# Expert jobs of a four-layer transformer kernel: the first matrices and the biases stand in SBUF, and ScalarE copies a job's matrix by a register

## The reference, cut to what matters

```python
def _L3_ffn_ref(x, Wg, bg, W1, b1, W2, b2):
    x_flat = x.reshape(N * T, d)                      # 2048 x 256, after a layer norm
    probs = jax.nn.softmax(x_flat @ Wg + bg, axis=-1)
    assignments = jnp.argmax(probs, axis=-1)
    h = jnp.einsum('nd,edh->neh', x_flat, W1) + b1[None]
    h = jax.nn.gelu(h, approximate=False)
    eo = jnp.einsum('neh,ehd->ned', h, W2) + b2[None]
    selected = jnp.take_along_axis(eo, assignments[:, None, None], axis=1)[:, 0, :]
    w = jnp.take_along_axis(probs, assignments[:, None], axis=1)
    return (w * selected).reshape(N, T, d)
x = x + _L3_ffn_ref(_layernorm(x, axis=-1), ...)
```

## Time and profile before

| | us |
|---|---|
| median of 3 runs | 1631.82 |
| lowest, highest | 1628.55, 1633.62 |
| the profiled execution | 1627.8 |
| its span in the trace | 1626.1 |

### The profile page before, as it was taken

One profiled execution on the slowest core, in us unless ns is written; L12 is line 12 of the kernel. 1 busy time (PEld: TensorE's weight loads), 2 busy tenths in 40 slices (PEclk: granted clock), 3 DMA queues, 4 the chain that ended last, 5 costly groups with the idle time before them and its releaser, 6 DMA issues.

```text
span 1626.1 us, 26351 instructions
## 1 busy us (share of the span) xinstructions
PE 1441.3 (89%) x9849; PEld 1075.0 (66%) x9849; DVE 1075.7 (66%) x2362; ACT 750.3 (46%) x1256; POOL 116.0 (7%) x168
## 2 busy tenths in 40 slices
PE   7999999878897996798889999999988899899557
PEld 5666666557783443477786878787864677788546
DVE  4456575778877775787766465555458988886344
ACT  2211212257773665476672222222224877788323
POOL 1000000000000000111000000000010001001323
PEclk9999999989998997999999999999998999999779
DMA  9462202320000000000008910000100000000155
GB/s 320 172 207 78 78 1 78 116 97 14 14 3 1 1 1 1 25 14 1 14 2 271 301 41 1 0 1 0 33 7 7 2 7 2 7 29 26 41 182 185
DMA packets 60286, 96.62 MB, mean 59 GB/s; under 512 B 11092, under 2 KB 48973, under 8 KB 59983
## 3 DMA queue, kind: packets, MB, share of 16 engines
q1 hardware_dynamic: 57742, 78.50, 15.0%
q10 hardware_dynamic: 544, 12.16, 2.2%
q0 software_dynamic: 1872, 4.27, 0.7%
HBM read 73.21 MB, written 37.30 MB: 68 GB/s over the span
## 4 chain that ended last, share of the span: by engine, by line
PE 55%; DVE 17%; issue 11%; ACT 6%; DVEq 5%; DMA 2%; SPq 2%; ACTq 1%; POOL 1%; POOLq 1%
PE bank L2013 8%; PE bank L2014 8%; PE bank L1703 7%; PE bank L1681 7%; DVE MB L928 3%; PE bank L1808 3%; DVE plo L946 3%; PE bank L1859 2%; PE bank L1779 2%; PE bank L1741 2%; PE bank L1781 2%; PE bank L1609 2%; PE bank L1812 2%; PE bank L1813 2%; DVE raw L1223 1%
## 5 line engine op out<-in xcount | busy, mean ns | idle before, releaser
L946 DVE TENSOR_TENSOR plo<-e,phi 120x512 f16<-120x512 f32 x256 | 180.0, 709 | 51.0 <-ACT phi L1431 46.9
L1425 ACT ACTIVATE e<-bank 120x512 f32<-120x512 f32 x256 | 150.5, 588 | 45.5 <-PE bank L1813 36.1
L928 DVE TENSOR_REDUCE MB<-bank 128x4 bf16<-128x480 f32 x256 | 156.2, 648 | 13.7 <-PE bank L1781 9.7
L1431 ACT ACTIVATE phi<-e 120x512 f16<-120x512 f32 x256 | 161.3, 630 | 8.6
L1356 ACT ACTIVATE act<-bank,bin 127x512 f32<-127x512 f32 x64 | 43.1, 686 | 167.3 <-DVE dec L758 163.2
L1681 PE MATMUL bank<-xT,winT 128*127 128x512 f32 (+1 forms) x256 | 114.6, 593 | 1.3 <-ACTq L1327 1.3
L1703 PE MATMUL bank<-woutT,msk 128*128 128x256 f32 (+1 forms) x512 | 115.2, 379 | 0.0
L677 DVE TENSOR_SCALAR high<-raw 128x512 int32<-128x512 int32 x96 | 41.0, 427 | 107.9 <-ACT raw L1562 60.8
L1703 PEld LDWEIGHTS bank<-woutT,msk 128*128 128x128 f32 (+1 forms) x512 | 96.9, 190 | 15.4
L2013 PE MATMUL bank<-hah,h1w 128*128 128x512 f32 x256 | 101.3, 396 | 3.3 <-DVE hal L680 3.3
L557 POOL TENSOR_TENSOR veps<-mv,ceps 128x4 f32<-128x4 f32 x32 | 8.8, 276 | 1335.4 <-DVEq L648 1203.0
(11 more groups left out here) (309 smaller groups left out, 3519.3 us busy)
## 6 DMA issues: line engine op xcount, KB each, us to landing
copy_routed<-zeros SPq DMA_DIRECT2D x1, 17028.0 KB
jw<-copy_experts SPq DMA_DIRECT2D x23, 385.0 KB, 3.3
seen<-in_h1T SPq DMA_DIRECT2D x8, 512.0 KB, 7.2
seen<-in_h2T SPq DMA_DIRECT2D x8, 512.0 KB, 4.8
h1w<-copy_h1T SPq DMA_DIRECT2D x1, 4096.0 KB, 16.6
h2w<-copy_h2T SPq DMA_DIRECT2D x1, 4096.0 KB, 15.1
ctxp<-in_ctxT SPq DMA_DIRECT2D x13, 240.0 KB, 2.9
jx<-copy_routed SPq DMA_DIRECT2D x23, 132.0 KB, 3.2
```

Source lines behind the costliest of these rows:

```text
L928: dve.tensor_reduce(MB[:, t, h0 // 8, SK + h0 % 8:SK + h0 % 8 + 4], b[:, 0:4 * SK].rearrange("p (h k) -> p h k", h=4), AX.X, ALU.max).then ...
L946: dve.tensor_tensor(plo[:, g % 3, :], e32[:, g % 3, :], phi[:, g % 3, :], ALU.subtract).then_inc(s.lo, 1)
L1425: act.activation(e32[:, g % 3, :], bank[2 + g % 3][0:SK, :], ACT.Exp).then_inc(s.exp, 1)
L1431: act.activation(phi[:, g % 3, :], e32[:, g % 3, :], ACT.Copy).then_inc(s.phi, 1)
```

## The change

The expert kits in DRAM are gone, and with them `job_weights`. Instead all first matrices, first biases and second biases are loaded to SBUF next to the second matrices, in the same place of SP's list, by four more DMAs (two of 1 MB for the two halves of the first matrices, one of 8 KB in pieces of 8 bytes, one of 1 MB that repeats the second biases over the partitions). They use SBUF whose tenants are done by then.

Per job only the rows are transferred. The second bias is read in place: VectorE reads the expert's number from `jtab` into a register between `jxln` and `jres`, and `jres` reads `second_bias` by it. The first matrix (and first bias) is copied by ScalarE, SBUF to SBUF, to one of three fixed buffers `jw`: `job_first(j+1)` stands behind the gelu of job j-1, reads the expert's number to a register, and issues two copies of 128 x 258 and 128 x 256. TensorE's list in the loop is what it was, with the new names.

```diff
-            for k in range(K2):
-                sp.dma_start(kits[:, :, W1 + k * D:W1 + (k + 1) * D], a["w1e"][:, k * 128:(k + 1) * 128, :]).then_inc(Hf.zeroed, 16)
-            sp.dma_start(kits[:, :, B1:B1 + K2], a["b1e"].rearrange("p (e k) -> e p k", e=NE)).then_inc(Hf.zeroed, 16)
-            sp.dma_start(kits[:, :, B2:B2 + D], a["b2e"].unsqueeze(1).broadcast_to([NE, 128, D])).then_inc(Hf.zeroed, 16)
         for k in range(K2):
             sp.dma_start(experts[:, :, k, :], a["w2e"][...]).then_inc(ld_experts, 16)
+            sp.dma_start(firsts[k][:, :, 0:D], a["w1e"][:, k * 128:(k + 1) * 128, :].rearrange("e p n -> p e n")).then_inc(ld_experts, 16)
+        sp.dma_start(firsts[0][:, :, D:D + K2], a["b1e"].rearrange("p (e k) -> p e k", e=NE)).then_inc(ld_experts, 16)
+        sp.dma_start(second_bias[:], a["b2e"].unsqueeze(0).broadcast_to([128, NE, D])).then_inc(ld_experts, 16)
-        def job_weights(j, e):
-            sp.dma_start(jw[:, j % NB, :], kits[ds(e, 1), :, :].rearrange("e p n -> (e p) n")).then_inc(ld_job[j % NB], 16)
-            job_weights(j, sp.value_load(jtab[0:1, 1, j:j + 1], min_val=0, max_val=NE - 1))
...
             dve.tensor_scalar(jxln[:, b, :], jx[:, b, 0:D], ...)
-            dve.scalar_tensor_tensor(out=jres[:, b, :], in0=jw[:, b, B2:B2 + D], scalar=jx[:, b, D:D + 1],
+            e = dve.value_load(jtab[0:1, 1, j:j + 1], min_val=0, max_val=NE - 1)
+            dve.scalar_tensor_tensor(out=jres[:, b, :], in0=second_bias[:, ds(e, 1), :].rearrange("p o n -> p (o n)"),
...
+        def job_first(j):
+            if j >= NW:
+                act.wait_ge(Hf.act, j - NW + 1)
+            e = act.value_load(jtab[0:1, 1, j:j + 1], min_val=0, max_val=NE - 1)
+            for k in range(K2):
+                act.activation(jw[k][:, j % NW, :], firsts[k][:, ds(e, 1), :].rearrange("p o n -> p (o n)"), ACT.Copy)
...
+            job_first(0)
             for j in range(JOBS + 1):
                 if j < JOBS:
                     job_columns(j)
                 if j >= 1:
                     job_gelu(j - 1)
+                if j + 1 < JOBS:
+                    job_first(j + 1)
```

More of the change, by code:

```diff
@@ L40 @@
 OH = (NT - TT - 1, 2 * (NT - TT) - 1 + TT - 1)
-W1, B1, B2, KIT = 0, K2 * D, K2 * D + K2, K2 * D + K2 + D
+NW = 3
+W1ROW = (D + K2, D)
 class Layer:
@@ L176, in build @@
     jtab = put("jtab", [1, 2, JOBS], I32, at)
+    free_at = at[0]
     r2 = max(end1, at[0], r1 + 44192)
@@ L311, in build @@
     at = [r4]
+    second_bias = put("second_bias", [128, NE, D], F32, at)
     jx = put("jx", [128, NB, CELL], F32, at)
-    jw = put("jw", [128, NB, KIT], F32, at)
+    jw = [put(f"jw{k}", [128, NW, W1ROW[k]], F32, at) for k in range(K2)]
     jxln = put("jxln", [128, NB, D], F32, at)
@@ L323, in build @@
     experts = put("experts", [128, NE, K2, D], F32, at)
+    at = [r1]
+    firsts1 = put("firsts1", [128, NE, W1ROW[1]], F32, at)
+    at = [free_at]
+    firsts = [put("firsts0", [128, NE, W1ROW[0]], F32, at), firsts1]
+    assert at[0] <= r2 + 1024
     bank = [es.enter_context(nc.psum_tensor(f"bank{b}", [128, 512], F32)) for b in range(8)]
@@ L365, in build @@
     st_job = [sem(f"st_job{b}") for b in range(NO)]
-    LD_JOB = 2 * 16
+    LD_JOB = 16
+    LD_EXPERTS = (2 * K2 + 2) * 16
     TILES3 = PAIRS * HT
@@ L397, in build @@
     W_COPIED = 5 * 16
-    ZEROED = (1 + K2 + 2) * 16
+    ZEROED = 16
     LD_L2, LD_L3X, LD_L3 = (4 + 3 + 2 * 2 + 2) * 16, 4 * 16, 2 * 16
@@ L403, in build @@
     w_in["f3T"] = nc.dram_tensor("copy_f3T", [HID, D], F32, kind="Internal").ap()
-    kits = nc.dram_tensor("copy_experts", [NE, 128, KIT], F32, kind="Internal").ap()
     xbuf = nc.dram_tensor("copy_routed", [SLOTS, CELL], F32, kind="Internal").ap()
@@ L530, in _ @@
                             (ld_l1, LD_L1), (ld_l2, LD_L2), (mask_ready, (0, 16 * 5, 16 * 9)[sum(phases > q for q in (2, 4))]),
-                            (w_copied, W_COPIED), (ld_h1, PAIRS * LD_SEEN + 64), (ld_h2, 16 if phases > 5 else 0), (ld_experts, K2 * 16),
+                            (w_copied, W_COPIED), (ld_h1, PAIRS * LD_SEEN + 64), (ld_h2, 16 if phases > 5 else 0), (ld_experts, LD_EXPERTS),
                             (ld_l3x, LD_L3X if phases > 6 else 0), (ld_l3, LD_L3 if phases > 6 else 0),
@@ L1285, in job_input @@
                               ALU.mult).then_inc(Hf.norm, 1)
-            dve.scalar_tensor_tensor(out=jres[:, b, :], in0=jw[:, b, B2:B2 + D], scalar=jx[:, b, D:D + 1],
+            e = dve.value_load(jtab[0:1, 1, j:j + 1], min_val=0, max_val=NE - 1)
+            dve.scalar_tensor_tensor(out=jres[:, b, :], in0=second_bias[:, ds(e, 1), :].rearrange("p o n -> p (o n)"),
+                                     scalar=jx[:, b, D:D + 1],
                                      in1=jx[:, b, 0:D], op0=ALU.mult, op1=ALU.add)
@@ L1306, in _ @@
             job_table()
+            dve.wait_ge(Hf.tab, 1)
+            dve.wait_ge(ld_experts, LD_EXPERTS)
             for j in range(JOBS + 3):
@@ L1584, in job_gelu @@
                 last = act.activation(jh[:, j % 3, f, :], bank[j % 2][:, f * 128:f * 128 + 128], ACT.Gelu,
-                                      bias=jw[:, j % NB, B1 + f:B1 + f + 1])
+                                      bias=jw[0][:, j % NW, D + f:D + f + 1])
             last.then_inc(Hf.act, 1)
@@ L1592, in _ @@
             exponentials(1)
+            act.wait_ge(ld_experts, LD_EXPERTS)
+            act.wait_ge(Hf.tab, 1)
+            job_first(0)
             for j in range(JOBS + 1):
@@ L2112, in job_up @@
                 for k in range(K2):
-                    last = pe.matmul(bank[j % 2][:, tok(f)], jw[:, j % NB, W1 + k * D + f * 128:W1 + k * D + f * 128 + 128], jxT[:, j % 3, k, :],
+                    last = pe.matmul(bank[j % 2][:, tok(f)], jw[k][:, j % NW, f * 128:f * 128 + 128], jxT[:, j % 3, k, :],
                                      start=(k == 0), stop=(k == K2 - 1))
@@ L2132, in _ @@
             pe.matmul(bank[0][0:1, 0:NE], onesb[:, 0:1], acc[:, len(ROUTES), :], start=True, stop=True).then_inc(Hf.cnt, 1)
-            pe.wait_ge(ld_experts, K2 * 16)
+            pe.wait_ge(ld_experts, LD_EXPERTS)
             pe.wait_ge(Hf.tab, 1)
```

## The result

| | before | after |
|---|---|---|
| median, us | 1630.57 (6 runs, 1626.87 to 1633.62) | 1616.59 (6 runs, 1614.55 to 1618.8) |
| the profiled execution, us | 1627.8 | 1615.67 |
| its span, us | 1626.1 | 1613.9 |

The ratio after to before is 0.9908, with a 95% interval of 0.9892 to 0.9924. The change makes the kernel faster by 0.8 to 1.1%, some 14 us.

What follows compares the result with a forecast made beforehand. SP's two issues per job were taken to bound the job loop (2.453 us a job). Loop 8.0, start 0.8 and end 0.6 sum to 9.4 us, from 1631.8 to 1622.4 us; range 1618.0 to 1628.0.

Steps and rivals of the forecast that it cites:

- the term for the start: Loop start: second job's rows issued one SP slot (1.1 us) earlier, partly lost to TensorE's low clock; 0.8 us gained.
- the allowance of 0.06 us a job for a tie of VectorE and TensorE: Job loop: both engines at 1.97 us wait for each other and lose at irregularities, so 2.03 us a job.
- the step from the profiled execution to the median: Whole time: median of runs shown lies 4.0 us above the profiled execution, so 9.4 is taken from 1631.8.
- What bounds the kernel before: Job loop: SP's two issues per job set a 2.21 us floor; late landings and buffer waits add 0.24.
- The removed DRAM kits (0): Second layer's feed-forward, first pair: the kits' four copies ran beside busy TensorE; removal gives 0 us, at most 0.1.
- the early loads (0): Last attention: four added DMAs take some 12 to 20 us more, nobody waits; 0 us, bounded by 1.
- VectorE, L = 0.84 and a round of 1.97: VectorE in the loop: the register read makes L, from `jxln` to `jres`, 0.84 us and its iteration 1.97.
- TensorE, 1.97: TensorE in the loop: its list is unchanged, with a floor of 1.97 us a job.
- ScalarE's 1.8: ScalarE in the loop: register read and two copies make its round 1.8 us, at worst 2.1; hidden under 1.97.
- Rows land in 2.5: Row loads in the loop: without kits rows land in 2.5 us, the round may be 1.65; not a bound.
- The end, 0.6: After the loop: a 0.6 gap before U(21) goes, then GpSimd's last stores set the end; 0.6 us gained.
- The rivals: VectorE's read dearer, 1626.9 (0.17); rows late, 1629.4 (0.09); ScalarE bound, 1625.6 (0.08); read waits for empty engine, 1636.2 (0.04).

Runs made afterwards that it cites:

- a_down_half: Kernel after, with TensorE's second matmul of each job doing only the first of its two halves of hidden values (output differs); 1615.01 us, one execution.
- b_kit0_late: Kernel before, with job 0's kit issued after SP's wait for the scatters instead of ahead of it; 1630.9 us, one execution.
- a_extra_kit: Kernel after, plus a second register read and a second, kit-sized DMA (385 KB) per job on SP; 1630.55 us, ratio to before 1.0002.
- b_again2: Kernel before, unchanged, profiled a third time; 1630.42 us.
- b_again3: Kernel before, unchanged, profiled a fourth time; 1629.5 us.
- b_again: Kernel before, unchanged, profiled once more (its second profile); 1628.09 us.
- a_extra_small: Kernel after, plus a second register read and a second DMA of 1 KB per job on SP; 1624.5 us, ratio to before 0.9967.
- a_act_copy2: Kernel after, with ScalarE making each matrix copy twice, the first to buffers nobody reads; 1617.37 us, one execution.

## Why the prediction was right and where it was wrong

The mechanism was right: SP's two issues and the kits' bytes held the loop, and without them TensorE's own list sets the round. Of the 5.8 us between 1622.4 and 1616.59, three things are the main part: the term for the start (0.8, where the profiled executions have 2.4: 1.6), the allowance of 0.06 us a job for a tie of VectorE and TensorE that doesn't exist (1.0), and the step from the profiled execution to the median (3.1).

**What bounds the kernel before: right.** Late rows starved the loop, SP's two slots were its floor. The runs put numbers on both: 2.252 us a job with two slots and hardly any bytes, where the prediction had 2.21 plus 0.24 for everything else.

**The removed DRAM kits (0) and the early loads (0): no cost is shown.** The loads of the first matrices and first biases land 8.7 to 10.2 us after their issue, and that of the second biases, issued at 1468.73, 8.3 after it. So all are there about 18 us after the first issue at 1459.24, some 10 us later than the two alone; the estimate was 12 to 20. SP is done with the issues at 1471.5 instead of 1459.8 and still has some 81 us until the job table, where the earlier trace rows have 92.4. The gate step started 0.5 us later than in the profile of before, but so did the first of these issues, that for `experts`: it stands at 1458.79 before and at 1459.24 after. From there to the gate step pass 85.5 us before and 85.6 after. The four other kernels of before take 85.5 to 86.7, and the seven other edits of the kernel after that change nothing in between 85.5 to 86.8. So the loads lengthen the last attention by nothing that can be seen. That the first issue comes at 1458.7 to 1460.5 in the five profiles of kernels before and at 1458.7 to 1461.4 in the nine of kernels after shows no gain from the removed DRAM copies either.

**VectorE, L = 0.84 and a round of 1.97: wrong, and the main step that failed in the loop.** L is 0.43 in the median and the round 1.54. The step took TensorE's 0.84 because there too a read stands between two compute instructions. But there T(7) had been waited for, and the read could start only with it: 0.84 passed in the open. The same trace had the other case too. T(3) at 1568.48 had not waited, and its `up` followed 0.22 later, with the same read in between:

```profile
1568.70 1.12 PE L2113 MATMUL bank<-jxT,jw 128*128 128x128 f32 x8
```

On VectorE two instructions of 0.4 stand ahead, `jout` and `jxln`, and the read starts when the wait of the first is met (1578.3 against 1578.15). The row of `jxln` of job 0, which itself waited for its rows, shows the open price:

```profile
1559.23 0.41 DVE L1287 TENSOR_SCALAR jxln<-jx 128x256 f32<-128x256 f32 x1 [6.56 <-DMA jx<-copy_routed]
1560.28 0.48 DVE L1290 SCALAR_TENSOR_TENSOR jres<-second_bias,jx 128x256 f32<-128x256 f32 x1 [0.63 <-issue]
```

There L is 1.05, with the first and longest read of 0.548. The Trainium skill ("Perfetto Trace Analysis", section on the per-instruction lifecycle, on instructions of DVE and ACT) says that an instruction is pushed to a wait queue, where it waits for its semaphores, and that the sequencer is by then ready for the next. In this trace a read doesn't run ahead of an unmet wait: that of job 0 starts at 1559.3, behind the 6.56 us that `jxln` waited until 1559.23. The reads do run ahead of the engine once the wait is met.

**TensorE, 1.97: right.** 1.977, and it is the bound, as a_down_half shows.

**The 0.06 for two tied loops: wrong with L.** There is no tie; TensorE runs 32 us without a gap. The loop's forecast was 2.03 and 8.0 us; it measured 1.977 and 9.0. The allowance is worth 19 x 0.06 = 1.1 us, and the 1.977 in place of 1.97 takes 0.1 of it back.

**ScalarE's 1.8: too high**, about 1.4, for the same hidden read and since copies follow each other 0.31 apart, not 0.42. Nothing hung on it.

**Rows land in 2.5: it is 2.1** (2.0 to 3.3), and no bound, as said.

**The start, 0.8: of the terms of the sum the one that was wrong by the most.** Measured 2.4 to T(3), or 2.9 counted from the gate step. The pieces, from the issue of the last scatter (1553.01 before, 1553.50 after) to T(3): to the rows' issue 4.75 and 3.51, from there to T(0) 2.59 and 2.78, T(0) to U(0) 3.33 and 2.05, U(0) to T(3) 4.80 and 4.24. The first, 1.24, was missing altogether: the prediction did not ask what the removed kit of job 0 had run beside, which was the last scatter (1.5 us, b_kit0_late and a_extra_kit; 0.3 of it goes to a longer first register read on SP, 0.474 us at the longest). The third, 1.28, is the SP slot that was put at 1.1: T(1) follows T(0) by 1.36 instead of 2.63. The fourth, 0.56, is the clock: TensorE is busy from 1561.84 on, before from 1563.68, and is at 0.87 from 1564 to 1566, where the earlier trace rows have 0.50. All of it lies in U(1), 1.25 us against 1.81. The prediction had taken 0.3 off in case the clock came up at the same moment as before. In this run it came up earlier, after TensorE had begun U(0) earlier by 1.84.

**The end, 0.6: right**, 0.8.

**From the profiled execution to the median: 3.1 us of the miss.** Between the profiled executions the forecast was 9.4, and 12.1 were measured (12.2 between the spans), 2.7 short: 1.6 at the start, 1.0 in the loop, 0.1 at the end. The other 3.1 of the 5.8 between 1622.4 and 1616.59 come from the translation. The forecast subtracted from a median of three, 1631.8; with six runs it is 1630.57 (1.2). And the profiled execution of before lies 2.8 below its median, that of after 0.9 below (1.9). In the two first profiles of before the gate step came 1.6 to 1.9 us earlier than in b_again2 and b_again3, which is of that size. So the profiled execution that the forecast started from was an early one; whether that is the whole of it can't be told, since there is one profile of the unedited kernel after.

**The rivals.** None came. VectorE's read is 0.30 in the median, 0.548 at the longest, and not the bound. The floor of about 600 ns that the Trainium skill ("DMA: Bandwidth & Descriptors", section on latency and other measured facts) gives for it is not seen in these traces; the measurement decides. Rows don't land late, since what made them late was the kits. ScalarE has some 0.6 us of room. And no read waits until its engine is empty: L would have been 1.63, and even two reads make it 1.06 in the median.

## What to carry to other kernels

A register read between two compute instructions cost VectorE nothing in 18 of 23 jobs, in all but one of which about 0.8 us of its own work (`jout` and `jxln`) stood ahead of the read with its waits met, and some 0.6 to 0.7 us of idle engine where the instruction ahead was itself held up or a second read followed. Look where the sequencer's record starts, not where the read stands in the code, and take the price from a row whose instruction ahead was not waiting. When a transfer is removed, look in the trace at every transfer that was under way beside it, those of other queues too: 3.8 of the 9.0 us in the loop, and most of what the forecast of the start missed, were what the kits did to the landing of others. And a forecast that is added to a median needs to know on which side of it the profiled execution lies.

## What the runs showed of the hardware

- A 385 KB load that is issued beside an indirect scatter delays the scatter's landing by 1.5 us or more, in six profiles: 3.99 (before), 4.06 (b_again) and 4.13 (a_extra_kit) with it, 2.46 (after) and 2.46 (b_kit0_late) without, and 2.45 with a load of 1 KB (a_extra_small).
- 132 KB in 1056-byte pieces land in 2.1 us in the median without 385 KB loads beside them (after, a_extra_small), and in 3.2 with them (before, a_extra_kit).
- ScalarE's copies of 128 x 256 and 128 x 258 fp32 from SBUF to SBUF last 0.40 to 0.42 us each (after), but start 0.31 apart when they stand in a row (a_act_copy2).
- In the kernel after a register read takes 0.27 to 0.30 us in the median on SP, ScalarE and VectorE, and 0.38 on TensorE, where it was 0.30 before; the longest on each is 0.47 to 0.55. The longest of all runs is 0.78 (SP, a_extra_kit).
- The six loads in the last attention ran at 360 GB/s in the stretch 1466 to 1474, with TensorE's busy time from 1459 to 1530 no lower than before (60.6 and 60.2 us). In the stretch itself it was 6.3 of 8 us against 6.8, and the time from the first load's issue to the gate step was the same (85.6 and 85.5).
